# A fused token-mix and attention-cell kernel: stages of the late mixing halves placed at other steps, three of them with one projection product, weight folds after the prologue, DMA moves tied to steps, final norm on GpSimd

## The reference

```python
def _reference_tuple_inner(x, ...):            # block 1, behind a plain layernorm
    x = _layernorm(x, ln_g, ln_b)
    last_x = jnp.pad(x[:, :-1], ((0, 0), (1, 0), (0, 0)))
    k = (x * time_mix_k + last_x * (1.0 - time_mix_k)) @ Wk.T
    v = (x * time_mix_v + last_x * (1.0 - time_mix_v)) @ Wv.T
    r = (x * time_mix_r + last_x * (1.0 - time_mix_r)) @ Wr.T
    wkv = _wkv_scan(jnp.exp(k), v, jnp.exp(time_decay))   # running num / running den over tokens
    return jax.nn.sigmoid(r) * wkv @ Wo.T

for c in range(6):                             # block 2: six attention cells, 8 heads of 16
    q = ew[c, 0] * (nodes[in_q] @ We[eq] + be[eq])
    k = ew[c, 1] * (nodes[in_k] @ We[ek] + be[ek])
    v = ew[c, 2] * (nodes[in_v] @ We[ev] + be[ev])
    nodes[c] = act_w[c] * _mha(q, k, v, Wq[c], Wk[c], Wv[c], Wo[c]) + q
out = _layernorm(nodes[5], ln_g, ln_b)
```

## Time and profile before

| | us |
|---|---|
| median of 3 runs | 2386.11 (2385.42 to 2395.48) |
| the profiled execution | 2385.82 |
| its span, first to last instruction | 2384.0 |
| TensorE busy | 2283.3 (96%) |
| VectorE busy | 2052.0 (86%) |
| ScalarE busy | 1833.9 (77%) |
| GpSimd busy | 511.0 (21%) |
| mean granted TensorE clock | 0.971 |

### The profile page before, as it was taken

The page is one execution under the profiler, slowest core; times in us unless marked ns, Lnnn a source line. Parts: engine busy times, 40 slices in busy tenths (PEclk is TensorE's granted clock), DMA queues, the critical chain, the costliest instruction groups (busy, mean ns, idle before and its releaser), DMA issues.

```text
span 2384.0 us, 46323 instructions
## 1 busy us (share of the span) xinstructions
PE 2283.3 (96%) x18027; PEld 866.7 (36%) x18027; DVE 2052.0 (86%) x2271; ACT 1833.9 (77%) x3423; POOL 511.0 (21%) x644
## 2 busy tenths in 40 slices
PE   6699899999999999999999999999999999999996
PEld 3433333333333333333333333333333333333332
DVE  6687789998898998998998998988988888889883
ACT  3255778878788888888888888888888888688785
POOL 5321312213212202112112112112112112222201
PEclk9687999999999999999999999999999999899998
DMA  4230314323224224233233233133133124143201
GB/s 120 60 54 18 75 32 84 65 54 90 51 64 82 50 68 78 50 77 77 50 68 77 49 70 76 39 79 77 39 63 85 38 61 87 36 81 65 49 21 47
DMA packets 86521, 149.39 MB, mean 63 GB/s; under 512 B 34314, under 2 KB 48926, under 8 KB 86302
## 3 DMA queue, kind: packets, MB, share of 16 engines
q0 software_dynamic: 28224, 94.13, 19.2%
q1 hardware_dynamic: 58078, 52.30, 9.1%
HBM read 41.97 MB, written 14.91 MB: 24 GB/s over the span
## 4 chain that ended last, share of the span: by engine, by line
PE 84%; DVE 6%; ACT 5%; issue 2%; POOL 1%; DMA 1%; SPq 0%; POOLq 0%; ACTq 0%; DVEq 0%
PE ring L478 37%; PE context L526 32%; DVE max_neg L1007 3%; ACT e_ring L763 2%; PE wide L504 2%; PE ring L439 2%; PE ring L448 2%; PE ring L428 2%; PE ring L420 2%; PE ring L453 2%; ACT raw L776 2%; PE ring L348 1%; PE ring L349 1%; PE ring L329 1%; DMA rden_bc<-rden_dram 1%
## 5 line engine op out<-in xcount | busy, mean ns | idle before, releaser
L1007 DVE TENSOR_REDUCE max_neg<-wide 128x1 f32<-128x1024 f32 x1536 | 1843.6, 1220 | 247.3 <-PE wide L504 242.6
L763 ACT ACTIVATE e_ring<-ring 128x512 f32<-128x512 f32 x3072 | 1668.1, 596 | 342.5 <-PE ring L478 224.0
L504 PE MATMUL wide<-k_aug,q_aug 48*128 48x512 f32 x3072 | 1134.9, 451 | 12.8 <-DVE max_neg L1007 12.2
L478 PE MATMUL ring<-q_aug,k_aug 50*128 50x512 f32 x3072 | 1140.9, 450 | 1.3 <-ACT mixing_xT L627 1.1
L526 PE MATMUL context<-e_ring,v_aug 128*32 128x256 f32 (+1 forms) x10752 | 952.3, 426 | 23.6 <-ACT raw L776 23.4
L478 PEld LDWEIGHTS ring<-q_aug,k_aug 50*128 50x128 f32 x3072 | 465.8, 187 | 762.0 <-ACT e_ring L763 540.8
L504 PEld LDWEIGHTS wide<-k_aug,q_aug 48*128 48x128 f32 x3072 | 459.6, 188 | 36.1 <-DVE max_neg L1007 27.4
L526 PEld LDWEIGHTS context<-e_ring,v_aug 128*32 128x32 f32 x10752 | 214.5, 108 | 520.6 <-issue 357.7
L304 POOL DMA_DIRECT2D src<-node_dram x40 | 22.7, 568 | 675.8 <-PE ring L439 675.8
L1121 POOL TENSOR_TENSOR ctxT<-ctxT,rden_bc 128x1024 f32<-128x1024 f32 x23 | 54.8, 2385 | 309.1 <-DMA rden_bc<-rden_dram 309.1
L1104 POOL CAST q_part<-q_part 128x512 fp32r<-128x512 f32 x47 | 28.8, 613 | 361.0 <-ACT q_part L693 360.8
(11 more groups left out here) (226 smaller groups left out, 834.1 us busy)
## 6 DMA issues: line engine op xcount, KB each, us to landing
q_aug<-q_part POOLq DMA_DIRECT2D x138, 256.0 KB, 4.8
k_aug<-k_part POOLq DMA_DIRECT2D x138, 256.0 KB, 5.9
src<-node_dram POOLq DMA_DIRECT2D x40, 512.0 KB, 5.0
ctxT<-raw SPq DMA_DIRECT2D x384, 32.0 KB, 2.0
rden_bc<-rden_dram SPq DMA_DIRECT2D x23, 512.0 KB
node_dram<-node_ring SPq DMA_DIRECT2D x16, 512.0 KB, 2.9
q_aug<-rows_dram SPq DMA_DIRECT2D x192, 8.0 KB
node_ring<-in_L_attn_x SPq DMA_DIRECT2D x4, 512.0 KB, 5.0
```

The lines of the kernel that those rows point to most:

```text
L478: e.matmul(bk[:, :], k_aug[first:first + AUG, u % 2, h // 2, chunk * P:(chunk + 1) * P].bitcast(F32R), q_aug[first:first + AUG, u % 2, h / ...
L504: done = e.matmul(wide[w % 2][:, half_of(kh)], q_aug[first:first + SPLIT, u % 2, h // 2, q0:q0 + P].bitcast(F32R), k_aug[first:first + SPL ...
L763: e.activation(e_ring[:, n % E_SLOTS, :], bank[where["st", n]][:, :], ACT.Exp, scale=EXP_SCALE).then_inc(a_exp, 1)
L1007: e.tensor_reduce(max_neg[:, G % 2, row:row + 1], wide[w % 2][:, :], AX_X, ALU.max, negate=True).then_inc(v_mx, 1)
```

## The change

It has these parts.

1. *Stages placed anew*: `MIX_AT` gets other turns and steps for halves 2 to 7. The projections of half 4 go from steps -9 to -7 to steps 1 to 3, those of half 5 from -4 and -3 to 6, 8, 10. Apply and the transposes that follow it stand three to five steps apart in place of one.
2. *One product in place of two* for halves 3, 6 and 7 (`LERPED`): VectorE forms the difference of the tokens and the shifted tokens (LERP_D) and three mixes (LERP_K, _V, _R), and each projection is one product with unscaled weights (three more ScalarE copies at the start).
3. *Folds and the rest behind the prologue*: TURNS 36 to 33. Folds 1 to 5 go to steps -13, -12, -10, -8, -7, biases to -5, values of unit 0 to -4 and -3, and a load of ones on SP to step 4.
4. *Moves held to steps*: each move of q and k at step s waits until all scores before step s are issued (`p_st >= HG * s`). `normalise` waits for the square of group 3 of its own unit's numbering (`v_neg`, step 10). The first split of unit 0 on GpSimd waits for VectorE's second apply of half 1 (`v_n2`).
5. *Final norm*: statistics at 17 and 24, inverse at 18 and 25 on VectorE; rstd and apply at 19 and 26 and the affine part at 28 on GpSimd, store at 31 (unit 22's: 17/19, 18/20, 19/21, 22, 27).

```diff
-        w_time_t = sb("w_time_t", [P, 7, D])
+        w_time_t = sb("w_time_t", [P, 10, D])
...
+        LERPED = (3, 6, 7)
...
-        TURNS = 36
-        ORDER_AT, EDGES_AT, FOLD0_AT, UNIT0_AT, SPLIT0_AT, MOVE0_AT, FOLDS_AT, VALUES0_AT = 9, 15, 20, (22, 27), (25, 27), 28, 29, 31
+        TURNS = 33
+        ORDER_AT, EDGES_AT, FOLD0_AT, UNIT0_AT, SPLIT0_AT, MOVE0_AT = 9, 15, 20, (22, 27), (25, 27), 28
+
+        FOLDS_AT, BIASES_AT, VALUES0_AT, ONES_AT = (-13, -12, -10, -8, -7), -5, (-4, -3), 4
...
-            turns_then_steps((7, 7, 8, 17, 18, 21, 24, 24, 28, 29, 30, 30, 31, 31, 32, 33, 35), (-14, -14, -13)),
-            turns_then_steps((7, 8, 21, 23, 28, 29, 29, 29, 34, 35), (-14, -13, -12, -11, -11, -10, -9, -8, -8, -7)),
-            (-12, -11, -11, -10, -9, -8, -7, 2, 3, 4, 5, 7, 9, 11, 12, 13, 14, 15, 15, 16),
-            (-8, -7, -6, -5, -4, -3, -3, 13, 16, 17, 18, 20, 22, 23, 24, 26, 27, 28, 28, 30),
...
+            turns_then_steps((7, 7, 8, 17, 17, 17, 17, 17, 18, 21, 24, 24, 28, 29, 30, 30, 31, 31, 32), (-14, -13, -12, -12, -9)),
+            turns_then_steps((7, 8, 21, 23, 26, 26, 26, 26, 28, 29, 29, 29, 32),
+                             (-13, -12, -11, -10, -9, -9, -7, -6, -5, -5, -1)),
+            (-9, -8, -8, -4, -4, -4, -4, -4, 1, 2, 3, 3, 4, 5, 6, 7, 8, 10, 11, 12, 13, 14, 14, 17),
+            (-3, -2, -1, 4, 4, 4, 4, 4, 6, 8, 10, 10, 12, 13, 15, 16, 18, 19, 20, 22, 23, 26, 26, 30),
+            (U1 + 4, U1 + 6, U1 + 7, U1 + 10, U1 + 13, U1 + 13, U1 + 15, U1 + 15, U1 + 18, U1 + 19, U1 + 20, U1 + 20,
+             U2 + 13, U2 + 15, U2 + 30, U2 + 31, U3 + 4, U3 + 13, U3 + 14, U3 + 18, U3 + 30, U3 + 31, U4 + 1, U4 + 7),
...
+        def final_steps(u):
+
+            if u + 1 < LAST:
+                return (17, 24), (18, 25), (19, 26), 28, 31
+            return (17, 19), (18, 20), (19, 21), 22, 27
...
+                    if i in LERPED:
+                        e.wait_ge(v_lerp, 4 * LERPED.index(i) + n + 2)
+                        e.wait_ge(a_wt, 10)
+                        e.matmul(bk[:, :], w_time_t[:, 7 + n, :], (ek, ekv, er)[n], start=True, stop=True).then_inc(signal, 1)
+                    else:
...
+                if k == LERP_D and i in LERPED:
+                    e.wait_ge(a_xT, i + 1)
+                    e.tensor_tensor(y, xT[:, 1:BANK + 1], xT[:, 0:BANK], ALU.subtract).then_inc(v_lerp, 1)
+                if LERP_K <= k <= LERP_R and i in LERPED:
+                    n = k - LERP_K
+                    e.wait_ge(v_lerp, 4 * LERPED.index(i) + 1)
+                    e.scalar_tensor_tensor(out=(ek, ekv, er)[n], in0=y, scalar=col[:, C_MIX + n:C_MIX + n + 1], in1=xT[:, 0:BANK],
+                                           op0=ALU.mult, op1=ALU.add).then_inc(v_lerp, 1)
...
+                        first, sums, _, _, _ = final_steps(prev)
+                        if half == 1 and r in first:
+                            final_statistics(prev, first.index(r))
+                        if half == 1 and r in sums:
+                            n = 2 * CELLS[prev][1] + sums.index(r)
+                            if n > 0:
+                                e.wait_ge(g_fn, n)
+                            inverse(2 * B, (1.0, LN_EPS_OUT), v_fvar)
...
                 e.wait_ge(d_rden_in, DMA * (u + 1))
+                e.wait_ge(v_neg, (u + 1) * GPU + 3)
...
+                            e.wait_ge(p_st, HG * s)
                             move_q(e, unit, n)
...
+                        e.wait_ge(p_st, HG * s)
                         move_k(e, nxt, r - 8)
...
+                        if half == 0 and r in applied:
+                            hf = applied.index(r)
+                            y = last_y[:, half_of(hf)]
+                            e.wait_ge(v_fvar, 2 * CELLS[prev][1] + hf + 1)
                             power(2 * B, g_rsf)
+                            apply(y, y, 2 * B, g_fn)
...
                 if t == SPLIT0_AT[0]:
+                    e.wait_ge(v_n2, 2)
                     split_k(0, 0)
...
+                if (s, half) == (ONES_AT, 1):
+                    e.wait_ge(a_fold, NODES)
+                    load_ones(1)
```

101 lines of the change are left out of this document (44 added, 57 removed).

## The result

| | before | after |
|---|---|---|
| median of 4 runs, us | 2389.32 (2385.42 to 2395.48) | 2333.61 (2332.59 to 2336.67) |
| ratio after/before, 95% interval | | 0.9767 (0.974 to 0.9793) |
| span of the profiled execution, us | 2384.0 | 2331.2 |
| mean granted TensorE clock | 0.971 | 0.984 |
| first row maxima, us from the start | 71.98 | 62.75 |

The changed kernel is faster by 2.3%, 55.7 us by the medians and 52.8 by the spans. So close a hit is partly luck: the runs of the kernel before, from which it was counted down, spread over 10 us.

The account below looks back on a forecast made before the run. Plain units were taken as TensorE-bound with VectorE close behind, the gain lying in longer stretches and clock falls. Terms 7.5 + 9.5 + 7 + 9.9 + 2.9 + 15.6 + 2.0 = 54.4 us took 2386 to 2332, range 2314 to 2353.

Parts of the forecast that it names:

- Part 1: Prologue: first maxima at 64.5 in place of 71.98, with VectorE late next; gain 7.5 us, bounds 4 and 10.
- folds away, gain 7.5: Prologue: folds, values and biases leave TensorE's stretch ahead of the first maxima, which start 7.5 us sooner.
- Part 2: Lookahead: 52 us for 61.5, VectorE's floor 44.1 plus about 8 for folds, values and biases; gain 9.5 us.
- Part 3: Unit 0: six projections come in, GpSimd wait and clock fall go; 108 us for 114.8, gain 7, bounds 102 and 121.
- Part 4: Unit 1: held moves end the wait for normalise, half 6 loses products; gain 9.9 us. Unit 4 likewise, 2.9.
- Part 5: Final norm, units 20 and 22: VectorE rid of eight parts, rest spread; gain 15.6 us, most of it the clock.
- Part 6: Unit 23: normalise put behind the square no longer stands beside VectorE's small instruction; gain 2.0 us.
- Rival A: Clock falls once more in a dense place, unit 0, 20 or 22; 11 us, 2343 us; chance 0.22.
- Rival B: Shared-interface contention stretches half 3's mixes and L1012, and unit 20's fall returns; 2346 us; chance 0.10.
- Rival C: All clock falls go away: lookahead at 47, unit 0 at 103; gain 68, 2318 us; chance 0.13.
- Rival D: Slower: held k moves delay the spread in each of 22 units; 2405 us at 5 us later; chance 0.03.
- Rival E: Prologue and lookahead give nothing, as folds only move and half clock persists; 2349 us; chance 0.07.

Follow-up runs that it names:

- experiment 4: Changed kernel with folds 1 to 5, unit 0's values and the biases back in the prologue's last turns: 2327.74 us.
- experiment 5: Changed kernel with half 3 projected by two products again, halves 6 and 7 still by one: 2331.20 us.
- experiment 8: Changed kernel with the lookahead's transposes of halves 2, 3 and 4 one step behind their apply, in place of three or four: 2342.57 us.
- experiment 1: Half 4's TURN2: kernel before, step 18 for 16, plus normalise behind the square, 2371.78 us; changed kernel, step 15 for 17, 2349.56 us.
- experiment 7: Changed kernel with half 4's three projections back in the lookahead, steps -3 to -1 in place of 1 to 3: 2326.83 us.
- experiment 6: Changed kernel with halves 6 and 7 projected by two products again, half 3 still by one: 2338.92 us.
- experiment 3: Kernel before with only the change's final norm: 2400.85 us; run again, 2375.98 us, ratio 0.994.
- experiment 2: Kernel before with only the q and k moves held to their steps, without normalise's wait for the square: 2386.14 us.
- experiment 9: Changed kernel with folds, values, biases back in the prologue, half 4's projections at steps -3 to -1, half 3 by two products: 2326.96 us, ratio 0.9734.
- experiment 10: Kernel of experiment 9 with half 5 by one product too, its mixes at steps 5, 5, 7, 8 on VectorE: 2331.93 us.

## Why the prediction was right, and where it was not

The stretches gained 52.8 us for the 54.4 forecast, and the places were the right ones. But misses offset each other: the prologue gave 1.7 us more than forecast and the stretches without a forecast 1.0, unit 0 gave 2.6 less and the others together 1.7 less.

**Part 1, the prologue.** Size near (9.2 for 7.5), step wrong. I held VectorE to be next in line, with the reciprocals and the scan of half 3. It was the landing of the q moves, for which TensorE stood idle for 7.11 us. The forecast had considered this (landing estimated at 61.9) and then set the start later for VectorE. The 64.5 us were right for VectorE's first reduction, but the products of the maxima do not wait for it:

```profile
64.22 2.32 DVE L1029 TENSOR_REDUCE max_neg<-wide 128x1 f32<-128x1024 f32 x2
```

The step "folds away, gain 7.5" is the one that failed. With the single product as changed, the folds' return costs 1.8 us at the first maxima (64.57 for 62.75), or some 4.4 if the front of experiment 4 had been as late and slow as the changed kernel's; with two products it costs 9.4 (70.34 for 60.91), of which 1.2 are a later front. The contention of half 3's mixes was priced as "up to 2 us come back" and then left out of the sum: it is 1.1 to 1.3 us (experiment 5).

**Part 2, the lookahead.** Length forecast 52, measured 52.1, and two steps of the reasoning held on the chip: one-step distances bring back 8.5 us (experiment 8; the forecast had put these waits at 4.0 and two more such), and the floor of 44.1 that I worked out for VectorE shows up as a lookahead of 44.8 once the folds are gone (experiment 4). The "about 8 us above the floor" for the folds were 7.3. What I didn't draw from my own numbers is the sum of Parts 1 and 2 for the folds: 8 paid there for 7.5 gained here. How the gain of 9.4 divides is not shown: the distances give 9, the folds cost 7, half 4's projections gave 2, and those of half 5 were never put back into the lookahead.

**Part 3, unit 0.** The term that was mis-sized. The wait and the fall are gone for the reason given (experiment 1, both ways), but the unit took 110.4 us and not 108. The busy sum of TensorE came to 106.86 us, where 101.4 plus 5 for the lower clock had given 106.4. What I set too low is the idle rest, 3.5 us for 2. The waits for VectorE, for which I left the 2, took 0.9. A wait of 2.12 us at step 5 was in no term; it is for ScalarE's copy of half 5's transposes, which now stand at step 4, and ScalarE had itself waited 2.50 us for a small copy that VectorE makes ahead of it:

```profile
142.75 1.12 PE L437 MATMUL ring<-node_ring,w_k_fold 128*128 128x512 f32 x2 [2.12 <-ACT mixing_xT L645]
...
141.92 0.78 ACT L645 ACTIVATE mixing_xT<-ring,col 128x512 f32<-128x512 f32 x1 [2.50 <-DVE mixing_xT L854]
```

So VectorE's lag cost 3 us and not 2, in part by this way round.

More is to be learned from the place. Half 4's three projections, half of the 11.5 us, cost 8.1 us here and 2.1 at the end of the lookahead (experiment 7). The forecast counted what the move took from the lookahead and what it added here. It did not see that the gap which they leave is a wait of 1.77 us for VectorE, nor that the clock falls there and carries 0.50 into unit 0. I took the lower clock in the first steps as given ("as before"), and experiment 7 shows that it is not. Half 5's projections were not tested this way.

**Part 4, units 1 and 4.** 9.5 for 9.9 and 2.3 for 2.9. The holds are worth 6.1 by themselves in unit 1 (forecast 6.9), a half with one product 2.1 (forecast 2.85). The mis-sized term is 3 x 0.95 - 0. A projection of half 6 takes 1.92 us from its first product to the next score in experiment 6 (282.70 to 284.62) and 1.06 in the changed kernel (282.23 to 283.29), so a product is worth 0.86 us and a half 2.6. The other 0.5 may be what VectorE's four instructions, which I costed at nothing, take back; no run shows it. The forecast's own terms for unit 1, 6.9 and 2.85, give 9.75 and with the 0.7 for ScalarE 10.45; the 9.9 is neither sum.

**Part 5, the final norm.** 14.8 for 15.6 in the changed kernel, and 14.7 in the two units when done alone (experiment 3). The step "most of it the clock" held: no stretch at 0.50 in either unit, and 2.8 us less work on VectorE in unit 20.

**Part 6.** 2.2 for 2.0. The timelines of the changed kernel, unit 23, GpSimd's multiply and VectorE's next square:

```profile
2246.64 2.38 POOL L1148 TENSOR_TENSOR ctxT<-ctxT,rden_bc 128x1024 f32<-128x1024 f32 x1 [29.42 <-DVE max_turn L1047]
...
2245.68 0.18 DVE L1034 TENSOR_TENSOR max_part<-max_neg 128x16 fp32r<-128x16 f32 x1
2245.89 0.17 DVE L1038 TENSOR_TENSOR max_part<-max_neg,max_part 128x16 fp32r<-128x16 f32 x1
```

The multiply is now released by the transpose of the square, and the small instruction takes 0.18 for 2.31 us.

**Rival A** (the clock falls once more) did not happen; only the end of the lookahead's fall reaches 9.7 us into unit 0. Experiment 1 shows how near it is: two steps less and it costs 16.3 us, more than the 11 taken. **Rival B** is right in the prologue, 1.1 to 1.3 us, and wrong in units 20 and 22, where no first instruction of a square takes over 0.3 us. **Rival C** happened neither in the lookahead nor in unit 0 of this kernel, but experiments 4 and 7 come close to its values of 47 and 103, with 44.8 and 102.3. **Rival D** (slower by the holds) was right in its mechanism and failed in its size. In unit 10 the spread on SyncE's queue and the multiply and moves on GpSimd's are, in the changed kernel:

```profile
1070.88 0.63 SPq L1317 DMA_DIRECT2D rden_bc<-rden_dram  x1
...
1080.86 2.39 POOL L1148 TENSOR_TENSOR ctxT<-ctxT,rden_bc 128x1024 f32<-128x1024 f32 x1 [4.31 <-DMA rden_bc<-rden_dram]
1083.18 1.54 POOL L286 DMA_DIRECT2D k_aug<-k_part  x3
```

The spread does take longer beside the held moves: 10.0 us from issue to multiply, where in the kernel before it was issued at 1110.20 and released `normalise` at 1117.23, 7.0. But the stores ahead of it, issued 18.1 us into the unit in both kernels, had no moves in front. So the spread is issued 22.1 us into the unit in place of 25.7, and the multiply starts at 32.1 for 32.7. The other units are alike: in most of units 2 to 22 it is 9.4 to 9.5 us for about 7.0, and the multiply starts at 31.6 for 32.6. The spread loses 2.5 to 3 us, not the 5 that D feared, and 3.5 were won ahead of it. **Rival E** fell with the first score at 114.85.

What stays open: the exact share of the edit in the 5.4 us of experiment 4, whose kernel ran once; 1.3 of the 9.5 us of unit 1; and how the gain of the lookahead divides.

## What to carry to other kernels

A producer on a slow engine and the product that reads it need a distance in steps that covers the producer's whole duration: one misplaced pair cost 4 to 5 us of waiting, and 7 to 12 us more, most of it through TensorE's clock. Before moving work out of a stretch, ask which engine ends that stretch and what the gap does to the clock: six products cost 2.1 us where they filled a wait for VectorE and kept the clock up, and 8.1 in the unit that TensorE bounds. Changes that each look good in one stretch must be priced together with what they push on, as the folds and the single product of half 3 suggest. Before reading a microsecond out of a front, compare where the parts ahead of the edit stand.

## What the runs showed of the hardware

- A fall of the granted clock to 0.50 lasted 34.1 us while TensorE was busy for all 34.1 (experiment 1), and 27.2 with 26.87 busy in the kernel before.
- Nearly the same wait in unit 23 was followed by no fall in the profile of the kernel before (1.82 us), by 10.2 us at 0.50 in experiment 2 (1.77), and by 13.7 and 6.8 us in the two executions of experiment 3 (1.61 and 1.76).
- One execution on one core was granted 0.95 in its units where others have 1.00, and its plain unit took 90.80 us for 89.81 (experiment 3).
- A small VectorE instruction (128x16) beside a GpSimd multiply of 128x1024 took 2.1 to 2.3 us for 0.17 in four profiles, and each time ended within 0.05 us of the multiply's end (in experiment 2 the multiply ran from 2291.89 for 2.37 us, and the small instruction from 2292.04 for 2.26). So its price went by what was left of the GpSimd instruction.
- The clock at the start of unit 0 depends on what TensorE has at the end of the lookahead: 0.50 for 9 to 12 us in eleven profiles, 1.00 in the three in which half 4's projections stand there (experiments 7, 9, 10).
